# Two stacked graph layers over 128 graphs on one core: the program of every engine written out turn by turn, and another order of steps

## What is computed

```python
# layer 0 ("A" in the kernel): attention, mixed four times, then a layer norm
q = x @ Wq.T + bq; k = x @ Wk.T + bk; v = x @ Wv.T + bv          # 8 heads of 32
scores = jnp.where(adj == 0, -16384.0, einsum('bhnd,bhmd->bhnm', qh, kh))
pros = softmax(scores)
z = z_init = vh
for _ in range(4):
    z = 0.9 * einsum('bhnm,bhmd->bhnd', pros, z) + 0.1 * z_init
x = layernorm(x + z) * gamma + beta
# layer 1 ("B" and "C"): attention with an edge bias, then a feed-forward part of 1024
nx = ln(x, ln1_g, ln1_b)
q, k, v = nx @ wq + bq, nx @ wk + bk, nx @ wv + bv
scores = q k^T / sqrt(32) + where(adj > 0, 0.1 * adj * adj, -inf)
x1 = x + (softmax(scores) @ v) @ wo + bo
out = x1 + gelu(ln(x1, ln2_g, ln2_b) @ w1 + b1) @ w2 + b2
```

## Time and profile before

| | us |
|---|---|
| median of 3 runs | 2429.93 (2428.8 to 2429.98) |
| the profiled execution, its own time | 2428.21 |
| its span, first to last instruction | 2426.4 |
| PE busy | 2280.2 (94% of the span) |
| ACT busy | 1924.3 (79%) |
| DVE busy | 1718.6 (71%) |
| POOL busy | 1503.6 (62%) |
| mean granted TensorE clock | 0.989 |

### The profile page before, as it was taken

The page is one execution under the profiler, slowest core; times in us unless marked ns, Lnnn a source line. Parts: engine busy times, 40 slices in busy tenths (PEclk is TensorE's granted clock), DMA queues, the critical chain, the costliest instruction groups (busy, mean ns, idle before and its releaser), DMA issues.

```text
span 2426.4 us, 80248 instructions
## 1 busy us (share of the span) xinstructions
PE 2280.2 (94%) x29492; PEld 2164.7 (89%) x29492; DVE 1718.6 (71%) x7329; ACT 1924.3 (79%) x6462; POOL 1503.6 (62%) x1610
## 2 busy tenths in 40 slices
PE   2799999999999999999999999999999999999987
PEld 2689999999999999999999999999999999999986
DVE  2577777777767777767777767767767767776863
ACT  0678888888878888878888888878888888887964
POOL 0676666666666666666666666666666666666651
PEclk9999999999999999999999999999999999999999
DMA  3110010110011011011011011011011011011000
GB/s 93 34 33 30 27 37 24 32 37 30 26 37 29 26 37 36 19 36 37 19 37 36 19 36 37 19 37 36 19 37 36 19 37 36 24 32 36 19 15 14
DMA packets 95661, 76.63 MB, mean 32 GB/s; under 512 B 9601, under 2 KB 95105, under 8 KB 95361
## 3 DMA queue, kind: packets, MB, share of 16 engines
q1 hardware_dynamic: 95360, 71.87, 9.7%
HBM read 55.06 MB, written 16.78 MB: 30 GB/s over the span
## 4 chain that ended last, share of the span: by engine, by line
PE 84%; issue 4%; ACT 3%; DMA 3%; DVE 2%; POOL 1%; SPq 1%; POOLq 0%; ACTq 0%; DVEq 0%
PE ring_ps L337 36%; PE ring_ps L454 15%; PE ring_ps L400 12%; PE ring_ps L392 9%; PE score_ps L383 5%; PE ring_ps L420 5%; PE ring_ps L347 3%; DMA adj_A<-in_adj_dram 2%; ACT probs L490 1%; POOL x1b L774 1%; POOL rstd L759 1%; DVE n L667 0%; ACT hidden L518 0%; ACT hT_high L518 0%; DVE x L680 0%
## 5 line engine op out<-in xcount | busy, mean ns | idle before, releaser
L490 ACT ACTIVATE probs<-probs,negmax 128x128 f32<-128x128 f32 x2048 | 795.4, 395 | 11.7 <-DVE negmax L599 4.7
L750 POOL TENSOR_TENSOR probs<-probs,rinv 128x512 f32<-128x512 f32 x512 | 529.4, 1055 | 108.1 <-DVE rinv L613 108.1
L490 ACT ACTIVATION_READ_ACCUMULATOR probs<-probs,negmax 128x1 f32 x2048 | 395.8, 193 | 0.0
L504 ACT ACTIVATE zT<-ring_ps 128x512 f32<-128x512 f32 x256 | 158.3, 618 | 231.4 <-PE ring_ps L400 231.4
L337 PE MATMUL ring_ps<-inT_C_high,w_high 128*128 128x256 f32 x1024 | 301.3, 294 | 4.5 <-ACT hT_high L518 3.0
L392 PE MATMUL ring_ps<-ident,probs 128*128 128x128 f32 x2048 | 293.7, 276 | 7.2 <-POOL probs L750 4.5
L454 PE MATMUL ring_ps<-w_high,hT_high 128*128 128x256 f32 x1024 | 296.8, 290 | 0.9 <-DVE x L680 0.5
L673 DVE TENSOR_TENSOR hT_low<-hidden,hT_high 128x512 fp32r<-128x512 f32 x256 | 230.3, 900 | 87.3 <-ACT hT_high L518 83.4
L454 PE MATMUL ring_ps<-w_low,hT_high 128*128 128x256 f32 x1024 | 286.5, 280 | 0.0
L454 PE MATMUL ring_ps<-w_high,hT_low 128*128 128x256 f32 x1024 | 286.2, 279 | 0.0
L337 PE MATMUL ring_ps<-inT_C_high,w_low 128*128 128x256 f32 x1024 | 284.9, 278 | 0.0
(11 more groups left out here) (149 smaller groups left out, 7379.2 us busy)
## 6 DMA issues: line engine op xcount, KB each, us to landing
xT_sb<-in_xT_dram SPq DMA_DIRECT2D x64, 256.0 KB, 3.3
x_sb<-in_x_dram SPq DMA_DIRECT2D x64, 256.0 KB, 2.9
out_dram<-x SPq DMA_DIRECT2D x128, 128.0 KB, 1.7
adj_A<-in_adj_dram SPq DMA_DIRECT2D x64, 128.0 KB, 3.1
adj_B<-in_adj_dram SPq DMA_DIRECT2D x64, 128.0 KB, 2.1
probsT_A<-in_L_gnn_w_dram SPq DMA_DIRECT2D x1, 1024.0 KB, 7.7
probsT_B<-in_L_gnn_w_dram SPq DMA_DIRECT2D x1, 1024.0 KB, 10.1
probs<-in_L_gnn_Wq_dram SPq DMA_DIRECT2D x1, 256.0 KB, 2.8
```

Source lines behind the costliest of these rows:

```text
L490: e = act.activation(probs[:, u, h, :], probs[:, u, h, :], ACT.Exp, bias=negmax[:, u, h:h + 1], scale=-1.0, accum_out=sums[:, u, h:h + 1])
L504: act.activation(zT[k][:, :, :, :], ring(name).rearrange("p (b c n) -> p b c n", b=GB, c=C), ACT.Copy).then_inc(s_out[name], 1)
L750: pool.tensor_tensor(probs[:, u, hs, :], probs[:, u, hs, :], rinv[:, u, hs].unsqueeze(2).to_broadcast([P, HR, P]), ALU.mult).then_inc(s_pr ...
```

## The change

Three things are changed together; no arithmetic is, and each pair goes through the same 84 steps.

1. `run` writes out every turn. The class `Body`, which served both the written-out turns and the loop's (where the pair's number is a register), is gone; a `Timetable` lists all steps of all pairs once, gives each ringed step its bank and says which step it has to wait for. All semaphore counts are constants now.
2. `ORDER` is another table: the same 84 names in another order and with other lags. The largest is 6. The four mixing steps and `pv` stand as `z3 z0`, `z1` (behind `sA`), `z2 pv`; before, they stood as `z0`, `z1` (behind `sA`), `z2 pv`, `z3` (behind `sB`).
3. `wait_apart` with its tile `spare`, and `through` with its semaphore, are dropped.

```diff
 ORDER = """
-tC/5 eB10/4 xs/1 vB/4 z0/2 h3/3 eB11/4 y0/3 u0/5 rB1/4 wA0/2 h0/2 lx/2 u1/5 lt/0 eb/3 wA1/2 u2/5 msA/1 b1/4 c0/5 n0/3
...
+g/5 mB01/5 h2/4 pA11/3 n2/6 mB10/5 eB01/5 qA/2 mB11/5 kA/2 z3/4 z0/3 rB0/5 tC/6 eB10/5 vB/5 h3/4 i1/5 y0/4 h0/3 rB1/5
...
-RING_ORDER = [n for n in NAMES if KINDS[n][0] in RINGED]
-BANK = {n: i % RING for i, n in enumerate(RING_ORDER)}
...
+class Timetable:
+
+
+    def __init__(self, pairs):
+        self.steps = [(n, i - lag) for i in range(pairs + DEPTH) for n, lag in ENTRIES if 0 <= i - lag < pairs]
+        ringed = [s for s in self.steps if KINDS[s[0]][0] in RINGED]
+        scores = [s for s in self.steps if KINDS[s[0]][0] == "scores"]
+
+        self.bank = {s: i % RING for i, s in enumerate(ringed)}
+        self.before = dict(zip(ringed[RING:], ringed))
+        self.before.update(zip(scores[1:], scores))
...
-        def run(eng, steps):
-            head = DEPTH + 1 + (G - DEPTH - 1) % 2
-            for i in range(head):
-                steps(Body(i, G))
-            with eng.Fori(head, G - 1, 2) as i:
-                steps(Body(i, odd=head % 2))
-                steps(Body(i + 1, odd=(head + 1) % 2))
-            for i in range(G, G + DEPTH):
-                steps(Body(i, G))
...
+        def run(does):
+            for name, g in table.steps:
                 kind = KINDS[name]
                 if kind[0] in does:
-                    does[kind[0]](name, *kind[1:])
+                    does[kind[0]](name, g, *kind[1:])
...
-                def wait_apart():
-                    n = next(spares)
-                    dve.memset(spare[:, n:n + 1], 0.0)
...
-                def through():
-
-                    pool.sem_inc(s_through, 1)
```

More of the change, by code:

```diff
@@ L40 @@
 ORDER = """
-tC/5 eB10/4 xs/1 vB/4 z0/2 h3/3 eB11/4 y0/3 u0/5 rB1/4 wA0/2 h0/2 lx/2 u1/5 lt/0 eb/3 wA1/2 u2/5 msA/1 b1/4 c0/5 n0/3
[L42 to L45, removed]
+g/5 mB01/5 h2/4 pA11/3 n2/6 mB10/5 eB01/5 qA/2 mB11/5 kA/2 z3/4 z0/3 rB0/5 tC/6 eB10/5 vB/5 h3/4 i1/5 y0/4 h0/3 rB1/5
+eB11/5 c0/6 u0/6 n0/4 u1/6 xs/2 vA/2 laA/1 c1/6 wA0/3 laB/4 mA00/2 msB/5 c2/6 u2/6 c3/6 mA01/2 mA10/2 u3/6 sA/2 z1/3
+y1/4 pB10/5 pB00/5 eA00/2 pB11/5 h1/3 pB01/5 n1/4 wA1/3 eA01/2 lt/0 msA/2 d0/6 rA0/2 mA11/2 eA10/2 d1/6 tB/4 eb/4 i2/6
+st/6 b1/5 eA11/2 z2/3 lx/2 pv/5 pA00/2 rA1/2 kB/4 qB/4 pA01/2 xv/3 wB0/5 o/5 b2/6 i0/4 mB00/4 wB1/5 sB/4 pA10/2 eB00/4
+y2/5
 """
@@ new lines, in take, with emptied, by_parts @@
+            def take(name, g):
+                if (name, g) in table.before:
+                    old, h = table.before[name, g]
+                    pe.wait_ge(s_out[old], h + 1)
+            def emptied(g, of):
+                pe.wait_ge(s_out[of], g + 1)
+            def by_parts(dst, left, right, chunks):
+                pairs = [(kc, a, b) for kc in range(chunks) for a, b in ((0, 0), (0, 1), (1, 0))]
+                for n, (kc, a, b) in enumerate(pairs):
+                    mm = pe.matmul(dst, left(a, kc), right(b, kc), start=(n == 0), stop=(n == len(pairs) - 1))
+                return mm
@@ L458, in steps, with turn_back @@
-                walk(body, {"turn": turn, "project": project, "values": values, "scores": scores, "turn_probs": turn_probs,
-                            "hop": hop, "turn_back": turn_back, "attend": attend, "output": output, "up": up, "down": down})
-            run(pe, steps)
+                            emptied(g, f"pA{b}{half}")
+                mix(name, g, z[k - 1] if k else v_A[g % 2], probsT_A[g % 2])
+            def turn_back(name, g, k):
+                emptied(g, f"z{k}")
+                take(name, g)
+                for b in range(GB):
+                    for c in range(C):
+                        at = (b * C + c) * P
+                        mm = pe.transpose(ring(name, g)[:, at:at + P], zT[k][:, b, c, :], ident[:, :])
+                mm.then_inc(s_full[name], 1)
```

728 lines of the change are left out of this document (330 added, 398 removed).

## The result

| | before | after |
|---|---|---|
| median | 2429.95 us | 2375.32 us (2374.53 to 2376.84, 4 runs) |
| ratio to before, 95% interval | 1 | 0.9773 (0.9756 to 0.979) |
| span of the profiled execution | 2426.4 us | 2373.9 us |
| mean granted clock | 0.989 | 0.989 |

The kernel is 2.3% faster. The forecast was 2344 us with a range from 2324 to 2372: the sign was right, the gain was 55 us and not 86, and the time lies 3 us outside the range.

The account below looks back on a forecast made before the run. PE was taken to bound the kernel. First `d0` 165.0 + 59 x 34.74 (2049.7) + last four intervals 118.4 + end 7.2 = 2340.3 us of span, hence a median of 2344 us, range 2324 to 2372.

Parts of the forecast that it names:

- What bounds the kernel: Middle turns of 34.88 us are bound by PE alone; ACT still has 4.9 and DVE 8 us free.
- Part one, the loop: Writing out the turns removes 28 ends of rounds at 2.80 us, 78.4 us; nothing charged for fetching straight code.
- Part two, the waits: In the new order's turn PE never waits; no charge, upper bound 0.3 us a turn, 18 us in all.
- slack: Time to spare before PE would wait at the new turn's tight places; smallest 0.6 us, at `d0`.
- Part two, PE's own work: One entry into mixing less per turn, 34.88 to 34.74 us; all other PE steps the same.
- Part three, first turns: Start of the kernel: 4 us added for waits around the norm between layers, first `d0` at 165 us, bounds 155 to 180.
- Last turns: Last four `d0` intervals, where steps run out: 3 x 30.8 + 26.0 = 118.4 us, bounds 104 to 122.
- the ring: Chain `o`, norm, `tC`, `u`, `d1`, store, `o` that held the last intervals: 26 us, 30 with layer 1's exponentials.
- rival 1: A PE wait of 0.4 to 1.0 us in each turn takes the loop's place: 2368 to 2403 us; chance 0.12.
- Rival 2: Gaps at `tC` come from its input through POOL and DVE and outlive the loop: 2422 us; chance 0.04.
- rival 4: PE starves on straight code at instruction fetches, up to 2.0 us each; slower, 2580 us with two a turn; chance 0.04.
- Rival 3: First and last turns gain more: first `d0` at 155, last intervals of 104, 2320 us; chance 0.07.

Follow-up runs that it names:

- e1: The kernel before, old order kept, with only the hardware loop replaced by 69 written-out turns: 2349.94 us, ratio 0.9645.
- e3: The changed kernel with the unused 64-byte tile `spare` put back, so all tiles have their old addresses: 2349.17 us, ratio 0.9642.
- e4: The kernel before with only its order table replaced by the new one, still in the loop: 2504.85 us, ratio 1.0285.
- e5: The changed kernel with 64 unused bytes ahead of the first weight tile, so everything moves and no distance changes: 2375.5 us, ratio 0.9759.
- e8: The changed kernel with 64 unused bytes in front of the weights and 64 more at the old place of `spare`: 2348.92 us, ratio 0.9653.
- e11: The changed kernel with `spare` of 64 bytes put back and 128 more unused bytes ahead of `hT`: 2344.42 us, ratio 0.9633.

## Why the prediction was right or wrong

**What bounds the kernel: right.** PE alone bound the turn before and still does; DVE and ACT have as much free time as forecast.

**Part one, the loop: right.** 78.4 us were forecast; e1's span is 77.7 below that of before, and on one chip its median is 86.3 below. That the first of these agrees to a microsecond is in part luck: before itself moved by 6 us between the result and the runs beside e1. Taking nothing for the straight code held: no "issue" in the steady turns. Of the two queues the forecast spoke of one; the bytes it expected there, 4.6 to 5.2 MB, came over both (3.92 and 1.07).

**Part two, the waits: right.** No slack laid out by hand was used up: not one wait of PE in the 55 turns from 250 to 2200 us. POOL's wait for `adj_A` is gone, and it cost nothing.

**Part two, PE's own work: wrong, the step that failed.** "All other PE steps are the same ones" was true of the instructions, and the sum took it to be true of their durations. And the third item of the change was dismissed with "the dropped one-element writes and `through` lie on DVE and POOL beside PE's work and cost nothing". What the writes themselves cost can't be seen beside it; their tile's 64 bytes cost 0.40 us a turn, and that is what carried the result out of the range: with the tile back, e3 ran in 2349 us. Corrected by e3, the turn is 34.68 where 34.74 was forecast: the saving by the order is 0.20 us and not 0.14. The entry into mixing that was saved gave its 0.14 (pair 1.89, transposes behind scores 0.59). The projections gave another 0.14: `qA kA`, now neighbours, take 2.74, while in e1 they take 1.42 and 1.38, and `kB qB` 2.75 against 2.83. About 0.08 of it is lost again in `d0 d1` (5.69 against 5.66) and in four transposes ahead of `d0` (0.48 instead of 0.44). Nothing in the chain of before was read for why its two sorts of 12 matmuls took 1.38 and 1.42: there the size of the effect was visible, and a sum that ran over "the same" steps needed it.

**Part three, first turns: the step of +4 us was too small.** The first `d0` is at 173.97, with the tile too (e3, 173.67), and at 159.91 to 161.44 in all kernels with the old order: the order costs 12 to 14 us here, not 4. The stretches from 54 to 100 us and on to 174 of after:

```profile
54.00:100.00 46.00, 33.30 (x368) 29.54 (x368) 14.21 (x78) 23.40 (x86) 18.73 (x18) 0.81 0.11 33
100.00:174.00 74.00, 61.23 (x816) 55.83 (x815) 52.62 (x227) 50.97 (x184) 47.50 (x51) 0.91 0.08 23
```

and of before, to its first `d0`:

```profile
54.00:100.00 46.00, 34.11 (x452) 29.58 (x452) 20.21 (x110) 26.43 (x100) 22.20 (x22) 0.96 0.10 27
100.00:161.00 61.00, 54.06 (x730) 49.71 (x731) 44.92 (x208) 47.61 (x171) 44.63 (x47) 0.94 0.10 28
```

After, PE is idle for 25.5 of 120 us, before for 18.8 of 107: 6.7 more. And it is busy for 94.5 instead of 88.2 with about the same work (1184 and 1182 matmuls), 6.3 more. Its mean clock is 0.81 and 0.91 in the two stretches, where it was 0.96 and 0.94; busy time multiplied by the clock of its stretch gives an estimate of 82.7 us of work at the full clock after and 83.6 before, so the lower clock is enough to account for the 6.3. The forecast counted work at the full clock and called all the rest "holes", so it had no term for work at a lower clock. Two waits of PE carry the idle time:

```profile
PE ring_ps L298 <- DVE nx L606: 10.5, 2, 5.3
PE ring_ps L343 <- POOL probs L681: 9.8, 5, 5.6
```

The chain shows the first of them as the norm between the layers, from `y` to `tB`, twice:

```profile
100.21 0.70 DVE y L572
...
111.07 1.12 PE ring_ps L298 x4
...
129.21 0.69 DVE y L572
...
141.81 1.11 PE ring_ps L298 x4
```

10.9 and 12.6 us, where before had one of 9.5 on its chain. In between, DVE works through `v_A` and three steps of masks and maxima of layer 0 (`mA..`, 12 pieces of 0.20 us from 104.42 to 106.95), before it comes to the statistics of the second norm. In a full turn PE has other work under it; in the first ones it doesn't. That this is the cause of the 12 us is read from the chain; no run moved those entries alone.

**Last turns: mis-sized by 5.1 us.** 3 x 30.8 + 26.0 was forecast, 33.6, 31.8, 30.9 and 27.2 came: only the third met it. In the first of the four PE still has 30.3 us of work, which left 0.5 for waits, and it waits 3.3; the ring and the work don't hide each other fully. The layout has 1.9 of the 5.1, as e3 needs 121.6; that is what before took, 122.0. The new order gained nothing there.

**The rivals.** The time fell among those of rival 1, a wait in each turn, without that mechanism: no such wait exists. A number that lands where a rival put it does not confirm the rival; the trace has to show its wait. Rival 2 (gaps not the branch's) and rival 4 (PE starves on straight code) are refuted by e1: the same order without the loop has neither the gaps nor any other wait. Rival 3 (the ramps gain) has the wrong sign. The order gave back in the ramps the 12 us that it had won in the turns (59 x 0.20), and in the loop (e4) it is 2.85% slower than before. The range, 2324 to 2372, had bounds for waits and ramps and none for PE's own pace.

## What to carry to other kernels

When PE is busy without a hole, the next thing to read is how long the same instruction form takes in different places: two levels, as 1.38 and 1.42 here, are time that something other than the work decides; here the place of the tiles had a part in it. An edit that adds or drops a tile, however small, moves all tiles behind it; measure such edits apart, with a padding tile of the same size, before the rest of the change gets the credit or the blame. A gain per turn of an order must be set against its first turns at the lower clock, and the price of a loop's end read with one order does not hold for another. And when a rule is drawn from the length of a block, look at the steps inside it: a block of five steps hid here that three were fast and two slow.

## What the runs showed of the hardware that was not expected

- Where the tiles of PE's operands lie against each other in SBUF changes the pace of this kernel's 256-column matmuls: 113.3 to 114 ns at the low level, 117 to 120 otherwise. Moving all tiles behind the weights by 64 bytes is 26 us of 2375 (after and e3; e5 and e8 on one chip).
- The distance between the two operands (moving minus stationary, modulo 512) decides only in part. At 448 the low level is frequent, and at 0, 96, 128, 384 and 416 no step of the middle turns had it; but `vA` has it at 64 in e3, and `u2 u3` don't at 448, and with the same addresses `d` ran at 5.50 and at 5.69 us in different turns of one execution (e11).
- The end of a round of the loop cost PE gaps of 2.0 to 2.4 us with one order and of 2.6 to 4.9 with another, and more than the gap in all, 2.8 and 5.7 us in the mean. Behind a gap PE can be slower for a while: 1.08 us for the four matmuls of `tC` behind one gap of before, 0.63 behind another; in e4 the granted clock was 0.85 over the 10 us behind the gap at 819.16.
- The straight program of the changed kernel, 77820 instructions on all engines and 4.99 MB of code, showed no stall of PE for instructions from 250 to 2200 us.
